# Local-attention weights and tables loaded once, inverse norms by log, exp and a Newton step, and a pipelined setup of the distance attention

## The chip, the core and the metric

The kernel runs on one core of one Trainium2 chip. The metric is the device time of one execution in microseconds (us). A core has a matrix engine (TensorE, PE in the rows; PEld are its weight loads), a vector engine (DVE), a scalar engine (ACT), GpSimd (POOL), and SyncE (SP), which here only issues DMA transfers. Each engine works its instructions off in order; between engines the order is kept by semaphores.

## What is computed

The reference applies seven stages to an activation x of 4 batches of 1024 rows of 128 numbers. In short:

```python
x = x + ffn(norm(x)) / 2        # gelu feed-forward, 512 hidden
x = x + distance_attention(norm(x))   # 16 heads of 8; scores = -|q_i - q_j|^2 / sqrt(8)
x = x + ffn(norm(x)) / 2
x = x + local(norm(x)) / 2      # two layers of windowed attention + gated feed-forward
x = x + causal_attention(norm(x))     # 16 heads of 64
x = x + local(norm(x)) / 2
# inside one local layer (8 heads of 64, windows of 64 rows):
q = l2norm(q) * qs; k = l2norm(k) * ks
q, k = rotary_xpos(q, k)
h = a * gelu(g); x = x + h @ w2 + b2
```

The l2norm needs 16 inverse square roots per row (8 heads of q, 8 of k). The rotation is linear, so the kernel multiplies by the inverse norm after it.

## The kernel before, in words

`macaron` runs the stages one after the other. x stays in SBUF as 32 tiles of 128 rows (`c.X`). Each stage consists of blocks; at the end of a block all engines meet in a barrier, and `clear` is a barrier too.

**Feed-forward** (`gelu_ffn`, L93, run twice). A first block issues four weight loads on SP (L131 to L134). `row_statistics` (L51) is a block of its own. The main block goes in 8 steps of 4 tiles. POOL adds half of the bias to x (L145), and its loop ends with the last step; DVE adds the product (L160) and takes the moments (L45, L48), which is the last work of the block.

**Distance attention** (`distance_attention`, L230). Its setup has these blocks: weight loads; row statistics; the normalised and transposed x (`normalised_columns`: DVE L90, PE L1343, ACT L1354); and a block that makes q in both orientations, split in a high and a low part, and the squared norms (PE L318 to L347, ACT L356 to L367, DVE L376 to L391), batch by batch. Only in the next block does SP stack the operands of a group of four heads: 40 DMAs (L435 to L439) copy 8-row strips of `q_hi`, `q_lo` and `n_hl` into `query` and `keys`. There are two such sets of buffers, for even and odd units, and 16 units (4 batches x 4 groups) in all. A unit has 32 jobs: two score matmuls each (L466), one Exp over 128x1024 on ACT (L530), and the products with v (L481).

**Local layers** (`local_layers`, L601, run twice). Each run has two layers and works 64 tiles in 16 groups of four. The order of work is written out by hand: `over_steps` goes through steps, a step has four ticks r = 0 to 3, and in each tick an engine works for tiles at several lags. `own` is the tile of this tick, `last` the one before, `scored` is two ticks back (TQ), `turned` three (PT), `out` four (OT); a group's feed-forward (`ffn`) comes two steps later, its last product (`ending`) three. In one tick and in this order

- PE: q/k products (L945), transposes of the rotated rows (L961), values (L954), projection (L1015), mask and scores (L971, L977), transposes of the probabilities (L989), weighted values (L1004). In r = 2 the feed-forward's transposes (L1026) and two thirds of its up-products (L1039), in r = 3 the last third and the transposes of the next group's rows (L934), in r = 0 the down-products (L1047).
- ACT: squares (L1128), attention out (L1155), qT and kT (L1137, L1138), values (L1132), the transposed probabilities (L1151), Exp (L1147). In r = 3 it begins with two Gelu gates (L1164), and after kT comes the third gate and the load of the Exp table (L1186); then values and hT (L1122), which PE needs for the next q/k products. The Gelu table is loaded at the end of r = 2 (L1201).
- DVE: sums of the probabilities and their inverse (L1244, L1246), rotation (L1226 to L1228), squared norms (L1231), residual (L1251), row maxima and subtraction (L1237, L1239). In r = 3 the gated products (L1264), in r = 0 the group's result (L1271) and its row moments (L1256, L1260).
- POOL: scaling of the probabilities (L857), scaling of the rotated rows of `last` (L850); in r = 1 the deviations (L863 to L877) and the bias b2 (L882); then cosine plus sine part (L889), the floor (L894) and the power -1/2 of the squared norms (L896) of `own`.

The power is one instruction:

```python
pool.tensor_tensor(inv_norm[:], floored[:], minus_half[:].broadcast_to([P, 2 * HEADS]), ALU.pow)
```

At the start of a run of the local layers, ACT issues the loads of angles, scales and mask (L1101 to L1104) and then writes the first eight normalised tiles (L1109). SP loads the shifted rows of the first group (L783, L784, L796) and behind them 14 weight arrays (L830 to L836). POOL and DVE multiply the two rotation tables (L921, L1300), DVE casts the mask (L1297). PE transposes the first group (L934), ACT copies it to hT (L1122), and PE, DVE, ACT and POOL wait for all weights before their first tick.

## Time and profile before

| | us |
|---|---|
| median of 3 runs | 3575.77 (3573.64 to 3576.94) |
| profiled execution | 3580.72 |
| its span, first to last instruction | 3578.6 |
| PE busy | 3183.2 (89%) |
| ACT busy | 2167.5 (61%) |
| DVE busy | 1976.4 (55%) |
| POOL busy | 1737.4 (49%) |
| mean granted TensorE clock | 0.959 |

The profile shows one execution. In its rows, times are us from the span's start unless they are marked ns. A row of the timeline gives start, duration, engine, line and operation, and in brackets the idle time before it and what ended that. The stages of that execution: first feed-forward to 87, distance attention to 677, second feed-forward to 752, local layers to about 1540, causal attention to 2768, local layers to the end. The reading is the same for both runs of the local layers.

### The profile page before, as it was taken

The page shows a single profiled execution, that of the slowest core. Times are in us where ns is not written, and L with a number is a line of the kernel's source. Part 1 is how long each engine was busy: PE and PEld are TensorE (multiplying, and loading weights), DVE is VectorE, ACT ScalarE, POOL GpSimd, SP SyncE. Part 2 cuts the span into 40 slices and gives each one's busy share as a digit, 9 for nine tenths or more (in the row PEclk, how much of TensorE's full clock was granted, in tenths as well). Part 3 has the DMA queues.
Part 4 walks back from the last instruction along what each step waited for, and adds up shares of the span by engine and source line. Part 5 has one row for each costly group of instructions (what it writes and reads, how often), then busy time and mean ns, then how long its engine had stood idle before and what let it go on. Part 6 is the DMA issues. An engine that isn't in the chain of part 4 may idle for free. (4 is left out here: it accounts for less than half of the span.)

```text
span 3578.6 us, 73165 instructions
## 1 busy us (share of the span) xinstructions
PE 3183.2 (89%) x26564; PEld 1951.8 (55%) x26564; DVE 1976.4 (55%) x4014; ACT 2167.5 (61%) x3580; POOL 1737.4 (49%) x1412
## 2 busy tenths in 40 slices
PE   6499999868999999749999999999998599999995
PEld 5222222435666666526666666666665366666663
DVE  4200000337777777545556555656565577777773
ACT  2399999526666666535555555555554366666663
POOL 1100000039889988523333333333332698998882
PEclk9699999979999999979999999999999799999998
DMA  1122222021111111100000000000000211111111
GB/s 33 20 36 39 36 38 38 7 74 34 35 36 38 37 36 34 25 10 9 7 6 9 6 9 6 9 6 9 6 6 4 86 37 35 37 37 37 35 33 36
DMA packets 124405, 95.70 MB, mean 27 GB/s; under 512 B 80448, under 2 KB 100544, under 8 KB 123968
## 3 DMA queue, kind: packets, MB, share of 16 engines
q1 hardware_dynamic: 122784, 89.41, 11.4%
q10 hardware_dynamic: 1440, 3.80, 0.3%
q8 instruction: 122, 2.00, 0.2%
q14 instruction: 59, 0.48, 0.0%
HBM read 22.90 MB, written 2.10 MB: 7 GB/s over the span
## 5 line engine op out<-in xcount | busy, mean ns | idle before, releaser
L1761 POOL TENSOR_SCALAR e<-e,inv 128x768 f32<-128x768 f32 (+7 forms) x512 | 375.3, 746 | 761.8 <-DVE inv L1653 761.8
L1724 ACT ACTIVATE e<-e,nmax 128x768 f32<-128x768 f32 (+7 forms) x512 | 395.4, 772 | 429.5 <-DVE e L1648 426.2
L1648 DVE TENSOR_SCALAR_CACHE_REDUCE e<-slot 128x768 f32<-128x768 f32 (+7 forms) x512 | 376.2, 754 | 243.8 <-PE slot L1537 243.8
L530 ACT ACTIVATE e<-slot 128x1024 f32<-128x1024 f32 x512 | 472.9, 1091 | 43.8 <-PE slot L466 43.8
L896 POOL TENSOR_TENSOR inv_norm<-floored,minus_half 128x16 f32<-128x16 f32 x128 | 374.1, 2922 | 10.7
L1641 DVE COPY eT<-slot 128x512 f32<-128x512 f32 (+3 forms) x384 | 238.7, 622 | 234.1 <-PE slot L1548 233.9
L1548 PE MATMUL slot<-ident,e 128*128 128x128 f32 x2304 | 332.7, 280 | 8.7 <-POOL e L1761 3.7
L1531 PE MATMUL slot<-key,q 64*128 64x512 f32 (+3 forms) x1536 | 318.1, 518 | 19.0 <-ACT v L1711 12.7
L889 POOL TENSOR_TENSOR rot<-cosine,sine 128x1024 f32<-128x1024 f32 x128 | 302.1, 2360 | 44.3 <-DVE sine L1228 44.3
L857 POOL TENSOR_TENSOR prob<-prob,inv_total 128x1024 f32<-128x1024 f32 x128 | 242.6, 1895 | 129.2 <-DVE inv_total L1246 129.2
L1548 PEld LDWEIGHTS slot<-ident,e 128*128 128x128 f32 x2304 | 252.5, 141 | 92.0 <-issue 68.9
L945 PE MATMUL slot<-w_qk,hT 128*128 128x512 f32 x512 | 254.5, 621 | 35.7 <-DMA b<-in_local_b_dram 17.8
L481 PE MATMUL slot<-e,v 128*32 128x512 f32 x2048 | 280.6, 621 | 0.4 <-ACT e L530 0.4
L1563 PE MATMUL slot<-eT,v 128*64 128x256 f32 x2048 | 254.6, 385 | 0.9 <-DVE X L1664 0.9
L1151 ACT ACTIVATE probT<-slot 128x1024 f32<-128x1024 f32 x128 | 131.0, 1023 | 200.8 <-PE slot L989 200.8
L466 PE MATMUL slot<-query,keys 36*128 36x512 f32 x1024 | 211.2, 478 | 45.6 <-DMA keys<-n_hl 31.8
L850 POOL TENSOR_TENSOR rot<-rot,inv_norm 128x1024 f32<-128x1024 f32 x128 | 243.4, 1901 | 0.3
L449 POOL COPY v<-q_all 128x256 f32<-128x256 f32 (+1 forms) x16 | 6.3, 401 | 479.6 <-PE slot L481 455.9
L466 PEld LDWEIGHTS slot<-query,keys 36*128 36x128 f32 x1024 | 88.8, 190 | 270.7 <-ACT e L530 219.7
L541 DVE COPY oT<-slot 128x512 f32<-128x512 f32 x32 | 22.1, 691 | 371.5 <-PE slot L481 371.5
L1226 DVE TENSOR_TENSOR cosine<-slot,tables 128x1024 f32<-128x1024 f32 x128 | 155.3, 1213 | 116.4 <-ACT sq L1128 83.6
L1128 ACT ACTIVATE sq<-slot 128x1024 f32<-128x1024 f32 x128 | 130.0, 1016 | 132.0 <-PE slot L945 132.0
(161 smaller groups left out, 6420.8 us busy)
## 6 DMA issues: line engine op xcount, KB each, us to landing
v_mix<-v SPq DMA_DIRECT2D x256, 128.0 KB, 2.3
w_qkv<-in_causal_w_dram SPq DMA_DIRECT2D x32, 192.0 KB
query<-q_hi SPq DMA_DIRECT2D x128, 32.0 KB
keys<-q_hi SPq DMA_DIRECT2D x128, 32.0 KB
query<-q_lo SPq DMA_DIRECT2D x128, 32.0 KB
keys<-q_lo SPq DMA_DIRECT2D x128, 32.0 KB
hs<-H SPq DMA_DIRECT2D x32, 128.0 KB
h1s<-H SPq DMA_DIRECT2D x32, 128.0 KB
```

The lines of the kernel that those rows point to most:

```text
L466: m = pe.matmul(out[:, h, :], keys[k][p][rows, t * P:(t + 1) * P], query[k][p][rows, half * 512:half * 512 + 512], start=True, stop=True)
L481: m = pe.matmul(c.slots[3][32 * j:32 * j + 32, half, :], v[k][:, t, j, :], e[(n - 1 + j // 2) % E_RING][:, j % 2 * 512:j % 2 * 512 + 512], ...
L530: act.activation(e[n % E_RING][:], c.slots[n % RING][:].rearrange(flat), ACT.Exp, scale=2 * SCALE).then_inc(e_ready, 1)
L889: pool.tensor_tensor(rot[:, a.j, :, :].rearrange(flat), cosine[:], sine[:], ALU.add).then_inc(rot_ready, 1)
L896: pool.tensor_tensor(inv_norm[:], floored[:], minus_half[:].broadcast_to([P, 2 * HEADS]), ALU.pow)\
L945: m = pe.matmul(bank_qk[:, half, :], hT[:, a.j * P:(a.j + 1) * P], w_qk[a.depth][:, half * 512:half * 512 + 512], start=True, stop=True)
L1531: pe.matmul(c.slots[h][:, bank, 0:hi - lo], q[k][rows, i * P:(i + 1) * P], key[k][rows, lo:hi], start=True, stop=True)
L1548: m = pe.transpose(turn[:, bank, t * P:(t + 1) * P], e[n % RING][h][:, (at + t) * P:(at + t + 1) * P], c.ident[:])
L1563: m = pe.matmul(o[64 * h:64 * h + 64, place(one) // 4, place(one) % 4 * P:(place(one) % 4 + 2) * P], v[k][:, t, 64 * h:64 * h + 64], eT[pa ...
L1648: dve.tensor_scalar(e[n % RING][h][:, 0:cols], c.slots[h][:].rearrange(flat)[:, 0:cols], -1.0, None, ALU.mult, ALU.min, accum_out=nmax[:, ...
L1724: act.activation(part, part, ACT.Exp, bias=nmax[:, n, h:h + 1], scale=-1.0, accum_out=total[:, n, h:h + 1]).then_inc(e_ready, 1)
L1761: pool.tensor_scalar(part, part, inv[:, n, h:h + 1], 1.0, ALU.mult, ALU.mult).then_inc(scaled, 1)
```

## The change

- The local weights, rotation tables and mask are allocated once (`local_weights`) and filled in the second call of `gelu_ffn`: four more DMAs on SP in its first block, twelve on SP in its main block, and on POOL, behind its loop, the two tables and the cast of the mask. Both runs of the local layers lose their loads, table products and waits for them.
- b2 is no longer added by POOL: an unused row of the hidden layer gets the constant 0.0625 * gelu(16) = 1, and the matching row of w2 holds b2.
- The inverse norms: POOL floors the squared norms of `own` as before. One tick later ACT takes Ln and then Exp(-x/2) of them, behind squares (and, for r < 3, behind attention out) and ahead of qT and kT; POOL makes one Newton step of four small instructions, each waiting for the one before, ahead of the scaling of the rotated rows. The table that is loaded behind the third gate and before the first tick is now the set named `natural_log_exp_and_others`. No load is written out ahead of Ln in r = 3.
- The setup of the distance attention normalises, transposes and multiplies in one block, batch by batch, and SP stacks the first unit's 40 strips in that block, as soon as the first batch's parts exist. The stacking of the second unit starts with the next block, without a wait, as before.

The diff, cut to its core:

```diff
+def load_local_weights(sp, w, d, loaded, count):
+
+    for l in range(len(w.w_qk)):
+        for dst, src in ((w.w_qk[l], "w_qk"), (w.w_v[l], "w_v"), (w.w_o[l], "w_o"), (w.w1[l], "w1"), (w.w2[l], "w2"),
+                         (w.small[l], "small")):
+            sp.dma_start(dst[:], d[src][l]).then_inc(loaded, 16)
+    sp.wait_ge(loaded, count)
...
+                if ahead:
+                    sp.dma_start(angles[:], c.const["angles"]).then_inc(tables_loaded, 16)
+                    for l in range(2):
+                        sp.dma_start(scales[l][:], ahead_d["scales"][l]).then_inc(tables_loaded, 16)
+                    sp.dma_start(band_f[:], c.const["band"]).then_inc(band_loaded, 16)
...
                 with pool.Fori(0, STEPS) as i:
                     pool.wait_ge(x_ready, i + 1)
                     pool.tensor_tensor(x_b2[:], c.X[:, bass.ds(i * G, G), :], bias, ALU.add).then_inc(x_b2_ready, 1)
+                if ahead:
+                    pool.wait_ge(tables_loaded, 48)
+                    wide = "p t x y d -> p t (x y d)"
+                    for l in range(2):
+                        pool.tensor_tensor(ahead.tables[l][:].rearrange(wide), angles[:].rearrange(wide),
+                                           scales[l][:].rearrange("p x y d -> p (x y d)").unsqueeze(1).broadcast_to([P, TPB, 256]),
+                                           ALU.mult).then_inc(ahead_ready, 1)
+                    pool.wait_ge(band_loaded, 16)
+                    pool.tensor_copy(ahead.band[:].rearrange("p a n -> p (a n)"), band_f[:].rearrange("p a n -> p (a n)"))\
+                        .then_inc(ahead_ready, 1)
+
+            if ahead:
+                @block.sync
+                def _(sp):
+                    load_local_weights(sp, ahead, ahead_d, ahead_loaded, 192)
...
+                @block.sync
+                def _(sp):
+                    heads = [stack_head(sp, stacked, 0, 0, j) for j in range(GROUP)]
+                    sp.wait_ge(cleared, 5)
+                    sp.wait_ge(hi_ready, 1)
+                    for high, _, _ in heads:
+                        high()
+                    sp.wait_ge(lo_ready, 1)
+                    for _, low, _ in heads:
+                        low()
+                    sp.wait_ge(norm_hi_ready, 1)
+                    sp.wait_ge(norm_lo_ready, 1)
+                    for _, _, norms in heads:
+                        norms()
...
+                    def turn_rows(i):
+                        pe.wait_ge(xn_ready, G * (i + 1))
...
+                        m.then_inc(turned, 1)
...
+                    pe.wait_ge(loaded, 80)
+                    pe.matmul(c.slots[2][:, 0, 0:P], wv[:], wk[:], start=True, stop=True).then_inc(cross_ready, 1)
+                    turn_rows(0)
+                    turn_rows(1)
+                    pe.wait_ge(merged_ready, 1)
+                    pe.matmul(c.slots[2][:, 1, 0:P], merged[:], wo[:], start=True, stop=True).then_inc(eff_ready, 1)
+                    for b in range(B):
+                        columns(b)
+                        if b < B - 1:
+                            turn_rows(2 * b + 2)
+                            turn_rows(2 * b + 3)
+                        rows(b)
+                        norms(b)
...
-                            norm_out(b - 1)
-                    norm_out(B - 1)
+                        if b < B - 1:
+                            columns(2 * b + 2)
+                            columns(2 * b + 3)
+                        act.wait_ge(norm_ready, b + 1)
+                        act.activation(n_hl[0:HEADS, b * S:(b + 1) * S], c.slots[2][0:HEADS].rearrange(flat),
+                                       ACT.Copy).then_inc(norm_hi_ready, 1)
+                        act.wait_ge(q_ready, b + 1)
+                        act.activation(q_all[:, b * TPB:(b + 1) * TPB, :, :].rearrange("p t h d -> p (t h d)"),
+                                       c.slots[0][:].rearrange(flat), ACT.Copy).then_inc(q_out, 1)
...
+                        dve.wait_ge(norm_hi_ready, b + 1)
...
-                def load_weights(l):
-                    sp.dma_start(w_qk[l][:], d["w_qk"][l]).then_inc(w_in_loaded[l], 16)
...
-                    sp.dma_start(small[l][:], d["small"][l]).then_inc(w_out_loaded[l], 16)
-                    sp.dma_start(b2[l][:], d["b2"][l]).then_inc(w_out_loaded[l], 16)
-
                 sp.wait_ge(cleared, 1)
                 load_hs(group(0, 0, None))
-                load_weights(0)
-                load_weights(1)
                 over_steps(sp, ticks)
...
+                def inverse_norms(a):
+
+                    first = first_inv[:, a.j % 2, :]
+                    pool.wait_ge(first_inv_ready, a.t + 1)
+                    if known(a.t, 1):
+                        pool.wait_ge(correction_ready, 2 * a.t)
+                    pool.tensor_tensor(inv_square[:], first, first, ALU.mult).then_inc(inv_square_ready, 1)
+                    pool.wait_ge(inv_square_ready, a.t + 1)
+                    if known(a.t, 1):
+                        pool.wait_ge(inv_norm_ready, a.t)
+                    pool.tensor_tensor(product[:], inv_square[:], floored[:, a.j % 2, :], ALU.mult).then_inc(correction_ready, 1)
+                    pool.wait_ge(correction_ready, 2 * a.t + 1)
+                    pool.sem_inc(correction_seen, 1)
+                    pool.tensor_scalar(correction[:], product[:], -0.5, 1.5, ALU.mult, ALU.add).then_inc(correction_ready, 1)
+                    pool.wait_ge(correction_ready, 2 * a.t + 2)
+                    if known(a.t, 2):
+                        pool.wait_ge(unit_ready, a.t - 1)
+                    pool.tensor_tensor(inv_norm[:, a.j % 2, :], correction[:], first, ALU.mult).then_inc(inv_norm_ready, 1)
+
                 def unit_rows(a):
                     pool.wait_ge(inv_norm_ready, a.t + 1)
                     pool.wait_ge(rot_ready, a.t + 1)
                     rows = rot[:, a.j, :, :]
-                    pool.tensor_tensor(rows, rows, inv_norm[:].unsqueeze(2).broadcast_to([P, 2 * HEADS, D]), ALU.mult)\
+                    pool.tensor_tensor(rows, rows, inv_norm[:, a.j % 2, :].unsqueeze(2).broadcast_to([P, 2 * HEADS, D]), ALU.mult)\
                         .then_inc(unit_ready, 1)
...
-                def inverse_norms(a):
+                def floor_norms(a):
                     pool.wait_ge(norm2_ready, a.t + 1)
                     pool.sem_inc(floor_ready, 1)
-                    pool.tensor_scalar(floored[:], norm2[:, a.j % 2, :], 1e-24, None, ALU.max).then_inc(floor_ready, 1)
-                    pool.wait_ge(floor_ready, 2 * a.t + 2)
-                    pool.tensor_tensor(inv_norm[:], floored[:], minus_half[:].broadcast_to([P, 2 * HEADS]), ALU.pow)\
-                        .then_inc(inv_norm_ready, 1)
+                    if known(a.t, 2):
+                        pool.wait_ge(correction_ready, 2 * a.t - 2)
+                        pool.sem_inc(floor_ready, 1)
+                    else:
+                        pool.sem_inc(floor_ready, 1)
+                    pool.tensor_scalar(floored[:, a.j % 2, :], norm2[:, a.j % 2, :], 1e-24, None, ALU.max).then_inc(floor_ready, 1)
 
                 def ticks(step, depth):
                     for r in range(G):
                         if turned := tile(step, r, PT, depth):
                             scale(turned)
                         if last := tile(step, r, 1, depth):
+                            inverse_norms(last)
                             unit_rows(last)
                         if r == 1 and (ffn := group(step, FFN, depth)):
                             deviations(ffn)
-                            add_b2(ffn)
                         if own := tile(step, r, 0, depth):
                             rotated(own)
-                            inverse_norms(own)
+                            floor_norms(own)
...
-                pool.wait_ge(tables_loaded, 48)
...
                 pool.wait_ge(cleared, 4)
-                pool.wait_ge(w_out_loaded[0], 80)
-                pool.wait_ge(w_out_loaded[1], 80)
                 over_steps(pool, ticks)
...
                 t1(group(0, 0, None))
-                pe.wait_ge(band_ready, 1)
-                for l in range(DEPTH):
-                    pe.wait_ge(w_in_loaded[l], 32)
-                    pe.wait_ge(w_out_loaded[l], 80)
                 over_steps(pe, ticks)
...
-                act.dma_start(angles[:], c.const["angles"]).then_inc(tables_loaded, 16)
-                for l in range(DEPTH):
-                    act.dma_start(scales[l][:], d["scales"][l]).then_inc(tables_loaded, 16)
-                act.dma_start(band_f[:], c.const["band"]).then_inc(band_loaded, 16)
...
+                def inverse_norms(a):
+                    act.wait_ge(floor_ready, 3 * a.t + 3)
+                    act.activation(log_norm2[:], floored[:, a.j % 2, :], ACT.Ln).then_inc(log_norm2_ready, 1)
+                    act.wait_ge(log_norm2_ready, a.t + 1)
+                    if known(a.t, 2):
+                        act.wait_ge(inv_norm_ready, a.t - 1)
+                    act.activation(first_inv[:, a.j % 2, :], log_norm2[:], ACT.Exp, scale=-0.5).then_inc(first_inv_ready, 1)
...
                             squares(own)
                         if r < 3 and out:
                             attention_out(out)
+                        if last := tile(step, r, 1, depth):
+                            inverse_norms(last)
                         if scored:
                             heads(scored)
                         if r == 3 and ffn:
                             gates(ffn, 2)
-                            act.preload_act_table(ACT.Exp)
+                            act.preload_act_table_set("natural_log_exp_and_others")
                         if own:
...
-                act.preload_act_table(ACT.Exp)
-                for l in range(DEPTH):
-                    act.wait_ge(w_out_loaded[l], 80)
+                act.preload_act_table_set("natural_log_exp_and_others")
                 over_steps(act, ticks)
...
                     if known(a.t, 2):
-                        dve.wait_ge(inv_norm_ready, a.t - 1)
+                        dve.wait_ge(floor_ready, 3 * a.t - 3)
                     dve.tensor_reduce(norm2[:, a.j % 2, :], sq[:].rearrange("p (h d) -> p h d", d=D), AX.X, ALU.add)\
...
-                dve.wait_ge(band_loaded, 16)
-                dve.tensor_copy(band[:].rearrange(flat), band_f[:].rearrange(flat)).then_inc(band_ready, 1)
-                dve.wait_ge(tables_loaded, 48)
...
-                for l in range(DEPTH):
-                    dve.wait_ge(tables_ready[l], 1)
-                    dve.wait_ge(w_out_loaded[l], 80)
                 over_steps(dve, ticks)
...
+    bias[:, 0, hid], bias[:, 1, hid] = 0.0625, 16.0
     down = np.zeros((n, chunks * P, P), w2.dtype)
-    down[:, :hid] = w2
+    down[:, :hid], down[:, hid] = w2, b2
...
-        gelu_ffn(nc, c, d["ffn_w1"], d["ffn_b1"], d["ffn_w2"], d["ffn_b2"])
-        local_layers(nc, c, local, moments=False)
+        weights = local_weights(nc, st, c)
+        gelu_ffn(nc, c, d["ffn_w1"], d["ffn_b1"], d["ffn_w2"], d["ffn_b2"], weights, local)
+        local_layers(nc, c, weights, moments=False)
         causal_attention(nc, c, d["causal_gain"], d["causal_shift"], d["causal_w"], d["causal_wo"], d["causal_bias"])
-        local_layers(nc, c, local)
+        local_layers(nc, c, weights)
```

## Rows read from the trace of the kernel before

**Rows 1.** Windows: busy time of each engine; one steady step, two ramp stretches of two ticks.
```profile
core 0: us, PE busy (x) PEld busy (x) DVE busy (x) ACT busy (x) POOL busy (x), PEclk, DMA share, GB/s
3166.10:3210.30 44.20, 41.76 (x430) 28.64 (x429) 33.73 (x48) 28.44 (x41) 39.78 (x26) 1.00 0.16 38
...
2845.30:2863.90 18.60, 15.56 (x191) 10.88 (x189) 14.97 (x18) 11.17 (x18) 18.43 (x12) 1.00 0.15 33
2863.90:2882.40 18.50, 17.33 (x198) 12.38 (x199) 13.99 (x18) 11.12 (x18) 18.33 (x11) 1.00 0.13 30
```

**Rows 2.** Timeline of PE in the steady step from 3166.1.
```profile
3170.03 0.66 PE L1026 MATMUL slot<-ident,z 128*128 128x128 f32 x4 [1.07 <-DVE H L1251]
3171.39 1.09 PE L989 MATMUL slot<-ident,prob 128*128 128x128 f32 x8 [0.71 <-POOL prob L857]
...
3177.43 1.95 PE L945 MATMUL slot<-w_qk,hT 128*128 128x512 f32 x4 [0.42 <-DVE hid L1264]
...
3186.49 1.96 PE L945 MATMUL slot<-w_qk,hT 128*128 128x512 f32 x4
```

**Rows 3.** Timeline of ACT in r = 3 of that step.
```profile
3182.01 0.69 ACT L1164 ACTIVATE gate<-slot,small 128x512 f32<-128x512 f32 x1 [0.59 <-PE slot L1039]
3182.72 1.28 ACT L1186 ACT_TABLE_LOAD   x1
3184.01 0.60 ACT L1132 ACTIVATE v<-slot 128x512 f32<-128x512 f32 x1
3185.81 0.60 ACT L1122 ACTIVATE hT<-slot 128x512 f32<-128x512 f32 x1 [1.20 <-PE slot L934]
```

**Rows 4.** Groups of POOL's instructions in the steady step 3122.0 to 3166.1.
```profile
L896 POOL TENSOR_TENSOR inv_norm<-floored,minus_half 128x16 f32<-128x16 f32 x4 | 11.7, 2924 | 0.3
L889 POOL TENSOR_TENSOR rot<-cosine,sine 128x1024 f32<-128x1024 f32 x4 | 9.4, 2359 | 0.0
...
L882 POOL TENSOR_TENSOR H<-H,b 128x512 f32<-128x512 f32 x1 | 1.3, 1277 | 0.0
...
L894 POOL TENSOR_SCALAR floored<-norm 128x16 f32<-128x16 f32 x4 | 1.0, 255 | 0.1
```

**Rows 5.** Timeline of ACT before the first local run: its nearest small instruction.
```profile
753.71 0.32 ACT L81 ACTIVATE deviation<-moments,eps 128x32 f32<-128x32 f32 x1
```

**Rows 6.** Timeline of the start of the first local run.
```profile
757.45 3.19 ACT L1109 ACTIVATE H<-X,x_shift,rstd 128x128 f32<-128x128 f32 x8 [3.41 <-issue]
...
771.11 0.60 ACT L1122 ACTIVATE hT<-slot 128x512 f32<-128x512 f32 x1 [10.48 <-PE slot L934]
...
780.06 3.75 PE L945 MATMUL slot<-w_qk,hT 128*128 128x512 f32 x4 [8.99 <-DMA b<-in_local_b_dram]
```

**Rows 7.** Timeline of the setup of the distance attention.
```profile
95.69 2.14 PE L1343 MATMUL slot<-ident,xn 128*128 128x128 f32 x8 [10.80 <-DVE xn L90]
...
105.68 0.77 PE L318 MATMUL slot<-wk,wv 128*128 128x128 f32 x2 [1.35 <-PEq L38]
...
136.55 1.21 DVE L384 TENSOR_TENSOR n_hl<-slot,n_hl 16x1024 fp32r<-16x1024 f32 x1 [4.35 <-ACT n_hl L356]
138.52 0.89 SPq L435 DMA_DIRECT2D query<-q_hi  x1
...
165.44 0.51 SPq L439 DMA_DIRECT2D keys<-n_hl  x1
...
167.26 1.65 PE L466 MATMUL slot<-query,keys 36*128 36x512 f32 x6 [31.79 <-DMA keys<-n_hl]
```

**Rows 8.** Windows of the distance attention, shortly after its start and later.
```profile
180.00:187.00 7.00, 7.00 (x32) 1.71 (x34) 0.00 (x0) 4.40 (x5) 0.00 (x0) 0.50 0.26 40
...
250.00:300.00 50.00, 48.49 (x340) 14.85 (x332) 4.78 (x12) 49.63 (x54) 0.80 (x2) 1.00 0.24 37
```

**Rows 9.** Timeline of the second feed-forward's end and the table product.
```profile
743.30 1.29 POOL L145 TENSOR_TENSOR x_b<-X,half_b 128x512 f32<-128x512 f32 x1 [6.16 <-DVE X L160]
...
752.41 1.28 ACT L78 ACT_TABLE_LOAD   x1 [5.88 <-PEq L38]
...
761.45 4.49 POOL L921 TENSOR_TENSOR tables<-angles,scales 128x2048 f32<-128x2048 f32 x1 [4.76 <-DMA scales<-in_local_scales_dram]
```

More of the change, by code:

```diff
@@ L90, in normalise, with local_weights, sb, gelu_ffn @@
     return dve.tensor_scalar(dst, c.X[:, t, :], c.moments[:, t, 0:1], c.rstd[:, bass.ds(t, 1)], ALU.subtract, ALU.mult)
-def gelu_ffn(nc, c, w1_d, b1_d, w2_d, b2_d):
+def local_weights(nc, st, c, depth=2):
+    HEADS, D, CH = 8, 64, 3
+    w = Ctx()
+    def sb(name, shape, dt=F32):
+        return st.enter_context(nc.sbuf_tensor(c.fresh(name), shape, dt))
+    w.w_qk = [sb(f"w_qk{l}", [P, 2 * HEADS * D]) for l in range(depth)]
+    w.w_v = [sb(f"w_v{l}", [P, HEADS * D]) for l in range(depth)]
+    w.w_o = [sb(f"w_o{l}", [P, HEADS // 2, P]) for l in range(depth)]
+    w.w1 = [sb(f"w1{l}", [P, 2, CH, P]) for l in range(depth)]
+    w.w2 = [sb(f"w2{l}", [P, CH, P]) for l in range(depth)]
+    w.small = [sb(f"small{l}", [P, 8]) for l in range(depth)]
+    w.tables = [sb(f"tables{l}", [P, TPB, 2, 2, D]) for l in range(depth)]
+    w.band = sb("band", [P, 2, 512], BF16)
+    return w
+def load_local_weights(sp, w, d, loaded, count):
[4 more added lines that the diff above has]
+    sp.wait_ge(loaded, count)
+def gelu_ffn(nc, c, w1_d, b1_d, w2_d, b2_d, ahead=None, ahead_d=None):
     HID = 512
@@ L125, in gelu_ffn @@
         moments_ready = sem("ffn_moments_ready")
+        if ahead:
+            angles = sb("angles", [P, TPB, 2, 2, 64])
+            scales = [sb(f"scales{l}", [P, 2, 2, 64]) for l in range(2)]
+            band_f = sb("band_f", [P, 2, 512])
+            tables_loaded = sem("tables_loaded")
+            band_loaded = sem("band_loaded")
+            ahead_loaded = sem("ahead_loaded")
+            ahead_ready = sem("ahead_ready")
         with nc.Block() as block:
@@ new lines, in norms @@
+                    def norms(b):
+                        pe.wait_ge(sq_ready, b + 1)
+                        if b:
+                            pe.wait_ge(norm_hi_ready, b)
+                            pe.wait_ge(norm_lo_ready, b)
+                        else:
+                            pe.wait_ge(merged_ready, 1)
+                            pe.wait_ge(eff_out, 1)
+                        for half in range(2):
+                            m = pe.matmul(c.slots[2][0:HEADS, half, :], sel[:], sq[b % 2][:, half * 512:half * 512 + 512],
+                                          start=True, stop=True)
+                        m.then_inc(norm_ready, 1)
@@ L359, in _ @@
+                    columns(0)
+                    columns(1)
                     for b in range(B):
[L360 to L362 removed]
                         act.wait_ge(qT_ready, b + 1)
```

172 lines of the change are left out of this document (77 added, 95 removed).

## The prediction

> **What bounds the kernel now.** The windows come first. In a steady step of the local layers PE is busy 41.76 of 44.20 us, POOL 39.78, ACT 28.44 [rows 1]. So PE leads, POOL follows closely, and at most 2.4 us a step can be won without taking work off PE. PE's timeline says what ends its idle times: 1.07 us by DVE's residual, 0.71 by POOL's scaling of the probabilities, 0.42 by the gated product [rows 2]; the rest, 0.24, by ACT. In the ramp (ticks 2 to 8, no feed-forward yet) two ticks take 18.5 to 18.6 us and POOL fills 18.4 of them, PE 15.6 and 17.3 [rows 1]: there POOL is the bound. The groups of POOL show why: the power costs 2.92 us a tile, 11.7 a step, for 16 numbers a row [rows 4]. Last come ACT's rows of r = 3, because the change puts work there: from the third gate to hT it has 0.59 and 1.20 us of idle time, and hT is done at 3186.41, right before PE's next q/k products at 3186.49 [rows 2, 3]. That copy is on the path, and has no slack beyond those 1.79 us.
>
> **Steady step, what goes.** POOL loses the power (11.7) and b2 (1.28) and gets 16 small instructions. The nearest row is the floor, 0.255 us on the same 128x16, and the next starts 0.08 after it: 0.335 each, 1.34 a tile, 5.4 a step. POOL falls to about 32 of 44 us. Of PE's waits only the 0.71 goes. The 1.07 stays: the residual of r = 2 sits behind the rotation, which waits for POOL's sum of r = 1, and there POOL begins when DVE hands it the inverse totals, with no power in between; b2's 1.28 leaves that stretch and 1.34 of Newton enters it. The 0.42 follows PE's own products through Exp, table load and gate, and stays. Gain 0.71.
>
> **Steady step, what comes.** In r = 3 ACT has the Gelu table when it meets Ln, and no load is written out for it; one has to be placed. Then Exp, then the third gate with Gelu again, then the named set. The edit names the set that holds both functions twice, which suggests that a function asked for by itself brings another: a load ahead of Ln, one ahead of Exp, one ahead of the gate. Three more loads of 1.28 [rows 3] and two small ACTIVATEs; these the trace does not show. Their bounds are nothing and the 0.42 or so of a wide one; the nearest row is 0.32 for 128x32 [rows 5]; I take 0.22 each. Together 3.84 + 0.44 = 4.3 us between squares and hT. The idle 1.79 absorbs its part, so hT is 2.5 us late; the transposes of the next rows are no way around it, since on DVE the residual waits behind the third gated product, which is late with the gate. PE waits for hT, and everything behind it in the step follows from PE. Minus the 0.71: +1.8 us a step. There are 14 steps a run with a feed-forward and own tiles, the last without a successor: 27 in all, +49 us. For r < 3 the two small instructions lie ahead of qT and kT, where ACT has idle time of their size (no price); if it had none, 3 x 0.44 would go on each step, which the range holds.
>
> A load is followed at once by the next ACTIVATE: 3182.72 + 1.28 = 3184.00, values at 3184.01 [rows 3]. The Trainium skill (ScalarE: Activation LUTs, What ACT_TABLE_LOAD costs) adds to the 1283 ns a drain of about 1380 ns for each switch of sets. By that rule the three loads would cost 8.0 us instead of 3.8; the row shows no such gap.
>
> **Ramp.** POOL per tick without the power and with Newton: 9.2 - 2.9 + 1.3 = 7.6 us. PE needs (15.56 + 17.33) / 4 = 8.2 [rows 1]; with the hops that remain, 8.5. Against 9.28 that is 0.8 a tick; 7 to 8 ticks a run, two runs: -12 us (0 if a chain between engines binds at once, -20 if PE's 8.2 falls too).
>
> **Start of a run of the local layers.** hT is complete at 771.71, the first q/k product runs at 780.06, held by the last weight array [rows 6]: 8.3 us go. ACT's first normalised tile stands behind the issue of four DMAs (3.41 us idle by issue, of which x_shift would hold it for half): 1.7 earlier. 10 us a run, the second alike: -20 (-16 to -24). PE is cold there before and after.
>
> **Second feed-forward, where the work goes.** SP issues four more loads in the first block, and a barrier waits for SP. The 40 stacking issues take 27.4 us, 0.69 each [rows 7]; plain ones are shorter, I take 2 us in all (0 to 2.8). The twelve weight loads lie beside 60 us of steps: nothing; should they be uncovered, a 10 us queue is what the old start showed. POOL's loop ends at 744.6; two tables at 4.49 and a cast (between 0.3 and the 2.36 of a two-operand instruction of its size [rows 4]; 1.4) end at 755.0. The block now ends near 751.7, 0.7 before the table load at 752.41 [rows 9]: +3.3 (+2 to +5). Sum +5.
>
> **Distance setup.** Now: transposes from 95.69, the next block from 105.68 to 137.76, 40 issues from 138.52 to 165.95, scores at 167.26 [rows 7]. Afterwards SP issues beside the products: q_hi of batch 0 exists about 8 to 9 us after 95.7, plus 27.4 gives 132. The engines need 32.1 us (the old block) plus between nothing and 32 x 0.27 = 8.6 for the transposes inside: 128 to 136. I take 133, barrier 0.8, scores at 134: -33 (-27 to -39). The second unit's stacking starts at 134 as well and needs 27.4 + 1.3; the first unit lasts 32 x 0.93 = 29.8 [rows 8]: just covered, so no further gain or loss. The long idle of PE (31.8) left it at the lower of its two levels, 1.2 GHz, until 187: five Exps in 7 us against 0.93 each later [rows 8], some 6 us lost. With a pause of 3 us left this may or may not go: half, -3. Sum -36. Moving b2 into w2 uses a padded row: nothing.
>
> **Sum.** -36 + 5 - 20 - 12 + 49 = -14. The profiled execution took 3580.7 (span 3578.6 and 2.1 around it), so 3567; it lies 5 above the median shown, and against 3575.8 that gives 3562.
>
> **Rivals.**
> 1. *Fewer loads.* If one load serves Ln and Exp, a step grows by 0.5: -14 - 27 x 1.28 = -49, 3527. If none is needed (a set that holds all, or ordering I misread), each step gains 0.71: -14 - 49 - 19 = -82, 3494. For: nothing in the trace of before shows which set Exp alone gets. Against: Gelu and Exp already cost two loads a step.
> 2. *Slower: the added chain is dearer than its instructions.* Each of the four Newton instructions waits for the one before. At 0.5 instead of 0.335 Newton takes 2.0, 0.7 more than b2 gave back on the path of r = 1; with Ln and Exp at 0.42, hT is later by another 0.4. Then a step grows by 2.9, 27 x 1.1 = 30 more: 3592. From a growth of 14 / 27 = 0.5 above my 1.8, at 2.3 a step, the change loses. For: nothing in the trace has four dependent small instructions. Against: the hop of 0.08.
> 3. *The drain of the skill's rule.* 3 x 1.38 x 27 = +112: 3674. The rows at two places a step show none.
> 4. *The setup's gain does not come*, because SP's strips or the second unit's stacking hold PE: -14 + 36 = +22, 3598.
>
> **How the numbers follow.** Forecast with three loads 0.54, its own range 3545 to 3582; one load for both 0.14; none 0.05; dear chain 0.18; setup held 0.07; drain 0.02. About 0.2% (7 us) can be told from no change. Of the forecast's 0.54, 0.37 lie below -7, 0.12 within it, 0.05 above. Faster: 0.37 + 0.14 + 0.05 = 0.56. Same: 0.12 and 0.06 of the dear chain, 0.18. Slower: 0.26. The range leaves out the case without loads, the drain and the tails: 3520 to 3600.
>
> **What would show it.** Right: three more table loads of 1.28 in each steady step, ahead of Ln, Exp and the third gate; hT right before the q/k products and PE's longest wait of the step there; steps of 46 us instead of 44.2; POOL near 32 a step; ticks of the ramp near 8.5; scores of the distance attention at 134; the first local q/k product 10 us after its block's start earlier than now, and the second feed-forward 5 us longer. Wrong: steps below 44 (fewer loads, or r = 3 has slack that I do not see), steps above 46.7, or Newton's four instructions taking over 1.8 us.

## The result and the profile after

| | before | after |
|---|---|---|
| median | 3574.65 (3573.64 to 3576.94, 6 runs) | 3559.87 (3558.11 to 3567.53, 6 runs) |
| ratio | | 0.9957 [0.9947, 0.9967] |
| span of the profiled execution | 3578.6 | 3556.3 |
| PE, DVE busy | 3183.2, 1976.4 | 3178.3, 1968.0 |
| ACT, POOL busy | 2167.5, 1737.4 | 2314.3, 1442.1 |

The change saves 14.8 us by the medians. The two profiled executions differ by more (spans 3578.6 and 3556.3), because the one of before took some 6 us more than its median and the one of after some 2 less. POOL loses 295 us of work, ACT gains 147. The sum is small because three gains (setup, b2, weights) and one large loss (the new norms) nearly cancel. All line numbers from here on are of the kernel after, unless a row is said to be of another.

The loads come first. ACT's groups after, over the whole span (group | busy us, mean ns | idle before):

```profile
L1310 ACT ACT_TABLE_LOAD x32 | 41.1, 1283 | 0.6
L1295 ACT ACT_TABLE_LOAD x32 | 41.1, 1283 | 0.6
L1250 ACT ACT_TABLE_LOAD x28 | 35.9, 1283 | 0.5
L1254 ACT ACT_TABLE_LOAD x28 | 35.9, 1283 | 0.5
L1271 ACT ACT_TABLE_LOAD x28 | 35.9, 1283 | 0.5
```

L1310 and L1295 are the two loads that the kernel before had too. Three more stand in each of 28 steps: at Ln, at Exp and at the third gate. ACT's timeline of r = 3 after, which answers to [rows 3]:

```profile
3143.79 1.03 ACT L1227 ACTIVATE sq<-slot 128x1024 f32<-128x1024 f32 x1 [1.51 <-PE slot L1053]
3144.84 1.28 ACT L1250 ACT_TABLE_LOAD   x1
3146.13 0.22 ACT L1250 ACTIVATE log_norm<-floored 128x16 f32<-128x16 f32 x1
3146.36 1.28 ACT L1254 ACT_TABLE_LOAD   x1
3147.66 0.21 ACT L1254 ACTIVATE first_inv<-log_norm 128x16 f32<-128x16 f32 x1
...
3148.86 1.28 ACT L1271 ACT_TABLE_LOAD   x1
3150.16 0.69 ACT L1271 ACTIVATE gate<-slot,small 128x512 f32<-128x512 f32 x1
3150.86 1.28 ACT L1295 ACT_TABLE_LOAD   x1
3152.16 0.60 ACT L1231 ACTIVATE v<-slot 128x512 f32<-128x512 f32 x1
3152.65 0.59 ACT L1221 ACTIVATE hT<-slot 128x512 f32<-128x512 f32 x1
```

ACT has no idle time from the load ahead of Ln to hT; the gaps of 0.59 and 1.20 us of before are used up. What PE waits for in the same step, from its timeline, which answers to [rows 2] (rows with a wait; one of 0.24 for ACT's attnT is left out, before and after alike):

```profile
3133.26 0.60 PE L1079 MATMUL slot<-band,ident_bf 128*128 128x512 bf16 x2 [0.66 <-ACT kT L1237]
3135.36 0.63 PE L1134 MATMUL slot<-ident,z 128*128 128x128 f32 x4 [0.46 <-DVE H L1358]
3141.80 1.96 PE L1053 MATMUL slot<-w_qk,hT 128*128 128x512 f32 x4 [0.16 <-DVE hid L1371]
3148.90 0.60 PE L1079 MATMUL slot<-band,ident_bf 128*128 128x512 bf16 x2 [0.81 <-ACT kT L1237]
3151.88 0.66 PE L1042 MATMUL slot<-ident,hs 128*128 128x128 f32 x4 [1.34 <-DVE H L1358]
```

The largest are in r = 3 and stand where the loads are: kT behind two of them (0.81), and the transposes for hT behind VectorE's residual (1.34), which stands behind the late third gate. The 0.71 for the probabilities is gone and the 1.07 has shrunk to 0.46. The wait of 0.66 in r = 2 is new, and comes up again below. POOL's busy time in a step fell from 39.78 [rows 1] to 30.37, as the windows show (columns as in [rows 1]):

```profile
3118.50:3164.30 45.80, 42.13 (x429) 28.57 (x428) 33.81 (x48) 33.52 (x51) 30.37 (x37) 1.00 0.15 35
```

The period of a step, from one result of a group on DVE (`H<-slot,H 128x512`) to the next, is the measure for everything below. It is the mean of the 26 full steps of an execution: 44.59 us before, 46.12 after.

The distance setup after, which answers to [rows 7], from the timeline (SPq rows are DMA issues):

```profile
104.72 0.91 SPq L329 DMA_DIRECT2D query<-q_hi  x1
...
130.98 0.50 SPq L339 DMA_DIRECT2D keys<-n_hl  x1
...
135.18 1.65 PE L584 MATMUL slot<-query,keys 36*128 36x512 f32 x6 [3.46 <-PEq L38]
```

And PE's clock around it, in the windows that answer to [rows 8]:

```profile
135.00:140.00 5.00, 3.89 (x12) 1.75 (x12) 0.00 (x0) 4.84 (x5) 0.74 (x2) 0.50 0.25 37
140.00:150.00 10.00, 10.00 (x60) 2.40 (x58) 0.00 (x0) 8.51 (x10) 0.00 (x0) 0.76 0.27 40
150.00:160.00 10.00, 10.00 (x68) 3.25 (x68) 0.99 (x3) 10.00 (x12) 0.00 (x0) 1.00 0.28 44
```

The granted clock was 1.00 from 125 to 131 us, where PE was busy 5.91 of 6 us, and 0.95 on the mean from 131 to 135. So even in a pause of 3.46 us PE came down to the lower level (0.50, 1.2 GHz), but the higher one was back some 10 us after the first score and not 20 as before.

The second feed-forward's end and the first start, which answer to [rows 6, 9], from the timelines of POOL, ACT and PE:

```profile
708.13 1.27 POOL L185 TENSOR_TENSOR x_b<-X,half_b 128x512 f32<-128x512 f32 x1 [6.18 <-DVE X L215]
709.36 8.98 POOL L190 TENSOR_TENSOR tables<-angles,scales 128x2048 f32<-128x2048 f32 x2
718.29 1.03 POOL L194 CAST band<-band_f 128x1024 bf16<-128x1024 f32 x1
```
```profile
720.11 1.28 ACT L78 ACT_TABLE_LOAD   x1 [8.73 <-PEq L38]
```
```profile
736.98 3.78 PE L1053 MATMUL slot<-w_qk,hT 128*128 128x512 f32 x4 [0.69 <-ACT hT L1221]
```

Put together, the profiled executions give this account. The marks are the last score, DVE's last product in the second feed-forward (749.80 before, 714.63 after), ACT's table load behind it, the first q/k product of each run (the second at 2803.96 and 2763.04), and the first and last group result of each run.

| stretch | measured, us | predicted, us |
|---|---|---|
| start to the last score of the distance attention | -35.8 | -36 |
| to the table load behind the second feed-forward | +3.5 | +5 |
| to the first q/k product of local run 1 | -10.8 | -10 |
| filling, to the first group result, run 1 | -4.2 | -6 |
| its steps | +21.1 | +24.5 |
| causal attention and the start of run 2 | -14.7 | -10 |
| filling, run 2 | -1.7 | -6 |
| its steps to the end | +20.3 | +24.5 |
| sum | -22.3 | -14 |

Of the 14.7, 11.0 lie between run 2's `deviation` on ACT and its first q/k product; the rest is spread over unchanged code. One execution is a draw for such stretches: the first score with the old setup came at 163.7 to 167.3 us in four profiles, with the new one at 134.8 to 140.1 in nine.

### The profile page after: what moved, and what is told of

The parts are those of the page before. It is cut to its first block and busy times, and to the rows that moved or that the text cites. A ratio compares the mean times of both kernels' runs of the same rounds, so it can differ in the third digit from the quotient of the medians.

```text
span 3556.3 us, 74663 instructions
## 1 busy us (share of the span) xinstructions
PE 3178.3 (89%) x26564; PEld 1944.6 (55%) x26564; DVE 1968.0 (55%) x4010; ACT 2314.3 (65%) x3920; POOL 1442.1 (41%) x1765
## 5 line engine op out<-in xcount | busy, mean ns | idle before, releaser
L648 ACT ACTIVATE e<-slot 128x1024 f32<-128x1024 f32 x512 | 472.5, 1087 | 11.8 <-PE slot L584 11.7
L1814 ACT ACTIVATE eT<-slot 128x512 f32<-128x512 f32 (+3 forms) x384 | 163.6, 426 | 74.2 <-PE slot L1644 72.6
L1351 DVE TENSOR_REDUCE total<-prob 128x8 f32<-128x1024 f32 x128 | 154.9, 1210 | 83.0 <-ACT prob L1246 83.0
```

Source lines behind the costliest of these rows:

```text
L648: act.activation(e[n % E_RING][:], c.slots[n % RING][:].rearrange(flat), ACT.Exp, scale=2 * SCALE).then_inc(e_ready, 1)
```

## The experiments

Each kernel is the one named with one edit, timed in rounds beside the kernel before. Theory at the start: the loss is the three table loads in r = 3, through hT; Newton's work takes b2's place on POOL. All periods are means of 26 steps. The step's differences are read within profiles and carry no interval of their own; the ratios do.

| kernel | median, us | ratio to before | step, us |
|---|---|---|---|
| before, four sets of runs | 3574.7 to 3576.1 | | 44.59 |
| after | 3559.87 | 0.9957 [0.9947, 0.9967] | 46.12 |
| e1 Ln and Exp behind the third gate | 3496.05 | 0.9773 [0.9757, 0.979] | 43.70 |
| e2 named set loaded ahead of Ln | 3527.92 | 0.9871 [0.9855, 0.9888] | 44.77 |
| e3 power on GpSimd again | 3483.92 | 0.975 [0.9734, 0.9767] | 43.06 |
| e4 old setup | 3589.78 | 1.0046 [1.0029, 1.0063] | 46.07 |
| e5 = e1, rotation first on POOL | 3477.71 | 0.9724 [0.9708, 0.9741] | 42.87 |
| e6 = e3, rotation first on POOL | 3499.31 | 0.9787 [0.977, 0.9805] | 43.58 |
| e7 before, b2 in w2 only | 3530.51 | 0.9873 [0.9856, 0.9889] | 43.02 |
| e8 before, weights ahead only | 3555.89 | 0.994 [0.9923, 0.9956] | 44.61 |
| e9 = e5, unit rows before the floor | 3474.42 | 0.9717 [0.9701, 0.9733] | 42.70 |
| e10 after, b2 on POOL again | 3605.78 | 1.0082 [1.0066, 1.0099] | 47.63 |
| e11 after, memsets later | 3560.71 | 0.9955 [0.9938, 0.9972] | 46.09 |

### The table loads: e1 and e2

```diff
@@ e1: ACT's ticks
-                        if last := tile(step, r, 1, depth):
+                        last = tile(step, r, 1, depth)
+                        if r < 3 and last:
                             inverse_norms(last)
...
                             act.preload_act_table_set("natural_log_exp_and_others")
+                        if r == 3 and last:
+                            inverse_norms(last)
@@ e2: ACT's ticks, ahead of inverse_norms(last)
+                            if r == 3 and ffn:
+                                act.preload_act_table_set("natural_log_exp_and_others")
```

> In r = 3, Ln and Exp of the inverse norms move on ACT behind the third gate and its table load, so no load has to be placed for them or ahead of the gate. Theory (three loads on the way to hT set the step): the three loads vanish from every steady step (28 each at three places, 84 in all), the step falls from 45.8 us to 43.5 to 43.9, and 27 steps give -50 to -60 against the changed kernel: 3500 to 3510 us. Rival (the Newton chain on POOL is what makes the step long): the loads vanish, but the step stays above 45 and the time within 15 of 3560, since POOL now gets the norms of r = 3 no earlier than before.

> The set with both functions is loaded by name ahead of Ln in r = 3: two added loads a step instead of three. Theory (the slack of 1.79 us on ACT is used up, each further load is paid in full): 1.28 x 27 = 35 less than the changed kernel, 3525 us, step 44.5. Rival (the step is limited by something beside ACT, the third load is partly hidden): less than 15 us gained.

e2 leaves two added loads of three and gains 32 us, 1.35 a step for a load of 1.28. e1 leaves none and gains 64, 2.42 a step. e2 held; in e1 the step held and the total came out 4 us below its range. In e1 the two small functions find their set loaded; ACT's timeline of its r = 3:

```profile
3148.01 0.69 ACT L1271 ACTIVATE gate<-slot,small 128x512 f32<-128x512 f32 x1 [0.59 <-PE slot L1147]
3148.71 1.28 ACT L1296 ACT_TABLE_LOAD   x1
3150.01 0.21 ACT L1250 ACTIVATE log_norm<-floored 128x16 f32<-128x16 f32 x1
3150.25 0.21 ACT L1254 ACTIVATE first_inv<-log_norm 128x16 f32<-128x16 f32 x1
3150.37 0.58 ACT L1231 ACTIVATE v<-slot 128x512 f32<-128x512 f32 x1
3151.81 0.60 ACT L1221 ACTIVATE hT<-slot 128x512 f32<-128x512 f32 x1 [0.86 <-PE slot L1042]
```

Three loads of 1.28 (3.85) cost 2.42: the difference is the idle time in r = 3 that they filled, which shows again as 0.59 and 0.86. The Trainium skill (ScalarE: Activation LUTs, Table sets: the hidden batching unit) counts one load for Ln followed by Exp. With the set named, e2 agrees: the load at L1291 (28 times) serves both. With the functions asked for alone, the kernel after shows two.

### The norms as a whole: e3

```diff
@@ POOL, floor_norms (not shown: ACT's inverse_norms and Newton's four instructions go, and the Exp table is loaded in place of the named set)
+                    pool.wait_ge(floor_ready, 2 * a.t + 2)
+                    pool.tensor_tensor(inv_norm[:, 0, :], floored[:, 0, :], minus_half[:].broadcast_to([P, 2 * HEADS]), ALU.pow)\
+                        .then_inc(inv_norm_ready, 1)
```

> The changed kernel with the inverse norms by the power on POOL again; the new setup, the weights ahead and b2 in w2 stay. Theory (the new norms cost 49 in the steps and give 12 in the ramp): 37 less than the changed kernel, 3523 us, steady step 44.1 or a little below since b2's 1.28 us on POOL are gone, ramp ticks 9.3. Rival (Ln, Exp and Newton are worth their place, the gain of the change comes from them): above 3560.

It missed by 39 us: 3483.92. The step is 43.06, 1.53 under the kernel before, though POOL still computes its powers. So something else that stayed in e3 was worth 1.5 us a step, and the new norms cost 76 us in all, 12 of them even without a load (e1 against e3). Only b2 was left as a cause in the steps.

### What b2 was worth: e7 and e10

```diff
@@ e7: POOL's ticks of the kernel before; e10 puts the same lines back into the kernel after
-                            add_b2(ffn)
@@ DVE, out
-                    dve.wait_ge(b2_ready, a.g + 1)
@@ local_layout
-    down[:, :hid] = w2
+    down[:, :hid], down[:, hid] = w2, b2
```

> The kernel before with one edit: the bias b2 comes into the second weight product as a row, and GpSimd's addition of b2 to the slot and its wait are gone. Theory (the addition of 1.28 us stood in GpSimd's chain of r = 1 that TensorE waits for, so it was worth its whole time in each of the 27 steps of a steady stretch, 35 us): 3540 us. The account behind the prediction, in which GpSimd had room for it once its place was free: within 10 us of the time before, 3565 to 3575 us.

> The kernel after with one part undone: b2 is added to the slot by GpSimd in r = 1 again, behind the deviations and ahead of the rotation. Chain account (whatever stands there delays the rotation, VectorE's residual and TensorE by its whole length, with Newton's four instructions ahead of it as without them): 1.3 to 1.6 us a step, 3595 to 3602 us. Rival (the three table loads set the step now, and the chain on GpSimd has room behind them): within 10 us of the kernel after, 3560 to 3570 us.

e7 gains 45.6 us, 1.57 a step on the mean, 10 us more than the chain account said and far from the other one. In most of the steps the gain is close to the 1.28 of the addition: 1.2 to 1.3 us in seven of the 13 of run 1, 1.4 to 1.5 in four. In the first and the twelfth it is 2.8, and the traces were not followed there. In e7's r = 1 POOL's rotation stands directly behind the deviations. Of the kernel before, DVE's rotation in r = 2 shows the link, a wait of its own of 0.71 for POOL's sum of r = 1; in e7 DVE's same instruction has no such wait:

```profile
3166.23 1.22 DVE L1226 TENSOR_TENSOR cosine<-slot,tables 128x1024 f32<-128x1024 f32 x1 [0.71 <-POOL rot L889]
```

PE's rows with a wait in e7's step (its own line numbers): of [rows 2], the 1.07 is now 0.23 and the 0.71 is 0.31, together 1.24 less. The 0.42 is as before.

```profile
3126.90 0.66 PE L1018 MATMUL slot<-ident,z 128*128 128x128 f32 x4 [0.23 <-DVE H L1243]
3127.86 1.09 PE L981 MATMUL slot<-ident,prob 128*128 128x128 f32 x8 [0.31 <-POOL prob L856]
3133.89 1.95 PE L937 MATMUL slot<-w_qk,hT 128*128 128x512 f32 x4 [0.42 <-DVE hid L1256]
```

The way back is as dear: e10 costs 45.9 us over the kernel after, 4 more than the upper end expected, in spite of the three loads (it also loads the two arrays of b2 again, beside the second feed-forward). The wait it lengthens is the new one of r = 2, from 0.66 to 1.77:

```profile
3124.42 0.60 PE L1088 MATMUL slot<-band,ident_bf 128*128 128x512 bf16 x2 [1.77 <-ACT kT L1246]
```

The chain is the same with a new end. POOL's floor stands behind the rotation, ACT's Ln waits for the floor (1.24 in the kernel after, 2.36 in e10), and qT and kT stand behind Ln on ACT. ACT's and POOL's rows of the kernel after:

```profile
3131.77 0.22 ACT L1250 ACTIVATE log_norm<-floored 128x16 f32<-128x16 f32 x1 [1.24 <-POOL floored L1012]
```
```profile
3123.87 0.22 POOL L952 TENSOR_TENSOR inv_square<-first_inv 128x16 f32<-128x16 f32 x1
3124.17 0.22 POOL L956 TENSOR_TENSOR product<-inv_square,floored 128x16 f32<-128x16 f32 x1
3124.58 0.20 POOL L959 TENSOR_SCALAR correction<-product 128x16 f32<-128x16 f32 x1 [0.20 <-POOL product L956]
3124.97 0.22 POOL L963 TENSOR_TENSOR inv_norm<-correction,first_inv 128x16 f32<-128x16 f32 x1 [0.18 <-POOL correction L959]
3125.28 1.90 POOL L969 TENSOR_TENSOR rot<-rot,inv_norm 128x1024 f32<-128x1024 f32 x1
...
3129.03 2.36 POOL L1002 TENSOR_TENSOR rot<-cosine,sine 128x1024 f32<-128x1024 f32 x1
3131.48 0.26 POOL L1012 TENSOR_SCALAR floored<-norm 128x16 f32<-128x16 f32 x1
```

### POOL's order: e5, e6 and e9

```diff
@@ e5: POOL's ticks, on top of e1 (e9 also puts unit_rows(last) ahead of floor_norms(own))
+                        if own := tile(step, r, 0, depth):
+                            rotated(own)
                         if last := tile(step, r, 1, depth):
                             inverse_norms(last)
+                        if own:
+                            floor_norms(own)
+                        if last:
                             unit_rows(last)
                         if r == 1 and (ffn := group(step, FFN, depth)):
                             deviations(ffn)
-                        if own := tile(step, r, 0, depth):
-                            rotated(own)
-                            floor_norms(own)
```

> The late-logarithm kernel (3496 us) with GpSimd's work of a later step in another order: the sum of the rotation comes before the four Newton instructions of the last repeat, and the floor of the own norms before the unit rows. Nothing else differs. Theory (what is left of the price of the new norms is GpSimd's chain in r = 1: four Newton instructions of about 0.33 us each stand ahead of the rotation, which VectorE's residual waits for, and the floor that the logarithm waits for, the waits of 0.66 and 0.46 us in r = 2): both waits go, a steady step falls from 43.8 to about 43.0 us, and the whole is 3475 to 3485 us. Rival (the unit rows, which now come 1.3 us later, are what the transposes wait for, or GpSimd was not the bound): 3496 us or more.

> The kernel with the power on GpSimd (3484 us) with its rotation's sum ahead of the unit rows and the floor ahead of the power. Theory (GpSimd's order in r = 1 still delays VectorE's residual a little, the wait of 0.23 us for the third residual): 3470 to 3480 us. Rival (nothing on TensorE's path waits for GpSimd's order any more): 3484 us, no change; if the power's later place delays the attention's scores that wait for it, above 3490 us.

> The kernel with the late logarithm and the rotation first (3478 us), with one more exchange on GpSimd: the unit rows come before the floor of the own norms (0.25 us). Theory (in r = 2 of a steady step TensorE waits 0.67 us for the unit rows, and they follow the floor directly): 0.25 us of it goes in each step, 3470 to 3475 us. Rival (the floor, 1.9 us later, makes the logarithm late, and ScalarE holds the copies of q and k behind it): 3485 us or more.

e5 held, 3477.71, 0.83 us a step under e1: both waits of r = 2 that it named are gone, and one of 0.67 for the unit rows has come. With the power on POOL the same order loses (e6, 3499.31): the rival's second branch has the number right, but not the reason. PE's wait for the scaled probabilities is 0.65 where e3 has 0.32. The power's later place is not what makes it: in both orders the same POOL instructions, the power among them, stand between one scaling of the probabilities and the next. In e6 the rotation comes first and POOL idles 0.30 ahead of it for DVE's sine part, so that from scaling to scaling it takes 11.65 us instead of 11.31. POOL's and PE's rows of e6, then PE's of e5:

```profile
3082.74 2.36 POOL L1002 TENSOR_TENSOR rot<-cosine,sine 128x1024 f32<-128x1024 f32 x1 [0.30 <-DVE sine L1331]
```
```profile
3094.14 1.09 PE L1095 MATMUL slot<-ident,prob 128*128 128x128 f32 x8 [0.65 <-POOL prob L976]
```
```profile
3116.93 1.09 PE L1071 MATMUL slot<-ident,rot 128*128 128x128 f32 x8 [0.67 <-POOL rot L969]
```

e9 exchanges 0.25 us and comes out at 3474.42, 3.3 us lower and inside what was expected. The intervals of the two ratios overlap, so the gain rests on the traces: the wait for the unit rows is 0.46 instead of 0.67, and the step 0.17 shorter. It is the fastest kernel of the study: 2.8% under before, 2.4% under after. So the change's way to make the norms beats the power where both were tried, by 9.5 us (e9 against e3), once its loads and its place in POOL's order are mended. Its steady step (windows) has less than 1 us left beside PE's own work:

```profile
3116.92:3159.28 42.36, 41.54 (x428) 28.59 (x428) 33.61 (x49) 29.64 (x49) 30.46 (x36) 1.00 0.17 39
```

### Setup and weights: e4 and e8

e4 takes the new setup out of the kernel after; e8 puts only the block ahead (four more loads on SP, fourteen weight loads with b2's two, POOL's two tables and the cast) into the kernel before.

> The changed kernel with the setup of the distance attention of before. Theory (the setup gives 33 by its start and some 3 by the clock): 36 more than the changed kernel, 3596 us, first scores near 168. Rival (the stacking only moves and binds later): less than 20 more.

> The kernel before with one edit: the local runs' weights, tables and mask are loaded and made once, beside the second feed-forward; the distance setup, the power and the addition of b2 stay. By the prediction's terms: 20 us off the two starts and 5 us on the second feed-forward, so about 3560 us. Rival (the starts are covered by TensorE's own clock rising and by other setup): no change, 3575 us.

The setup is worth 29.9 us, 6 less than expected. The score marks of all profiles agree with it. The first score comes at 165.9 (mean of four) against 137.1 (nine), 28.8 earlier, and the last one 31.2 earlier. The 35.8 of the pair before and after was a good draw for the new one. The weights are worth 20.3, 5 more than expected. Setup 29.9, b2 45.6 to 45.9 and weights 20.3 add up to about 96, against 91.5 measured for e3, which has all three. With the new norms' 76 taken off those 91.5, the 15 us of the result remain.

### A side observation: e11

```diff
@@ POOL, first block of the distance setup
                 def _(pool):
+                    pool.wait_ge(xn_ready, 4 * G)
                     for k in range(2):
```

> The kernel after with one wait added on GpSimd in the distance setup: its ten memsets (about 1 us each) start when VectorE has normalised the first 16 tiles, and not beside them. Theory (the memsets beside it made VectorE's normalising of eight tiles take 4.16 and 4.08 us where it took 2.14 us in the kernel before): both groups take 2.1 to 2.3 us again; the memsets and the first copies come later by 1 to 3 us, so the whole stays within 4 us of the kernel after, 3557 to 3565 us. Rival (the slow groups have another cause, such as the two halves of the buffer): they stay at 4.1 us.

DVE's rows of the kernel after, then of e11:

```profile
93.77 4.16 DVE L90 TENSOR_SCALAR xn<-X,moments,rstd 128x128 f32<-128x128 f32 x8 [0.73 <-PEq L38]
...
99.77 4.08 DVE L90 TENSOR_SCALAR xn<-X,moments,rstd 128x128 f32<-128x128 f32 x8
```
```profile
94.01 2.14 DVE L90 TENSOR_SCALAR xn<-X,moments,rstd 128x128 f32<-128x128 f32 x8 [1.01 <-PEq L38]
...
97.99 2.13 DVE L90 TENSOR_SCALAR xn<-X,moments,rstd 128x128 f32<-128x128 f32 x8
```

The theory held: beside the memsets the same eight instructions took twice as long. The total stayed where it was (3560.71). The first copy is issued at 104.72 in both profiles; in e11 it stands behind the fifth memset, which ends at 104.70, so what DVE wins is not passed on.

## Why the prediction was right

The mechanism of the loss, three table loads on the way to hT, was right and is shown by e1 and e2. That the total came within 2 us is partly luck: the steps cost less than taken, the filling and the setup gave less, the weights gave more, and these errors of 5 to 8 us partly cancel. The forecast gave b2 no worth of its own, and that was its largest mistake.

**Steady steps, what comes: right.** Three loads at the three named places, small functions at 0.21 to 0.22 as taken, 1.79 us of idle time used up. Taken: 2.5 us a step for all of it. Measured: 2.42 (after against e1) for the loads, with the small functions in both kernels. PE's longest waits were in r = 3, as forecast, but one stage ahead of hT's consumer: at the transposes (1.34) and the scores (0.81), not at the q/k products.

**What goes: the sum right, the terms not.** Predicted was a loss of the 0.71 only, with b2's 1.28 and Newton's 1.34 changing places in the chain of r = 1 at no gain. Measured: b2 gives 1.57 a step, Ln, Exp and Newton in place of the power take back 0.64 (e1 against e3), so 0.93 stays instead of 0.71. Newton is as long as thought (1.32 for the four, 1.41 to the next instruction), but only 0.86 of it is busy time, and so POOL is busy for 30.4 us a step and not 32. Why it costs less than b2 there was not tested by itself; that POOL reaches the probabilities earlier without the power would account for it (PE's wait for them is gone). Added up, -0.93 + 2.42 = +1.49, which is what the step shows (+1.53); taken was +1.8. The step missing from the prediction is the wait of r = 2: Ln waiting for POOL's floor with kT behind it. The prediction priced Ln and Exp for r < 3 at nothing because ACT has idle time there, and did not ask what they wait for; that wait is 0.66, and taking it away with its neighbour gave 0.83 a step (e5 against e1). The same oversight in another form spoiled the expectation of e3: b2 was held to be worth nothing by itself, though the prediction's own chain said that whatever leaves that stretch counts in full.

**Drain: refuted.** The prediction gave it 2 in 100. By the Trainium skill (ScalarE: Activation LUTs, What ACT_TABLE_LOAD costs) each switch has 1380 ns behind the 1283. The trace shows 1283 ns and the next instruction within 0.02 us (3146.36 + 1.28, then 3147.66), and a load taken away gave back 1.35, not 2.66.

**Filling: too large.** -6 instead of -12 in the profiles. No run was made for this stretch. Seven ticks, from the fourth q/k product to the eleventh, took 65.3 and 65.6 us before and 62.4 in both runs after: 8.9 a tick where 8.5 was taken, a gain of 0.4 instead of 0.8. The three ticks ahead of them ran partly at the lower clock and moved by -1.2 in run 1 and +1.1 in run 2. After the change POOL idles 5.5 us in 37 us of filling of run 2 (2815 to 2852), all of it waiting for DVE's inverse totals; so POOL is no longer the bound there, and a chain through DVE is the likely one.

**Starts and feed-forward: right.** Starts -10.8 and -11.0 (taken -10 each), feed-forward +3.5 (taken +5): +2.9 at POOL's tail and +0.6 in all that lies ahead of it, the issues among it.

**Setup: right in size, 6 us on the high side.** In the profiled pair the scores come 32 earlier, close to the 33 worked out; on the mean of all profiles it is 28.8, 4 less. From the first score to the last the new setup takes 481.3 us on the mean and the old one 483.7, 2.4 less against the 3 taken for the clock, but single profiles scatter by 8, so this term stays open. The high level did come back earlier after the short pause, but the lower one was still granted.

**Rivals.** Fewer loads: not in the kernel after, and e2 and e1 show the two cases at -32 and -64 us (from the prediction's 3562: 35 and 68). Dear chain: Newton's instructions cost 0.35 each with their hops (1.41 for the four), and the step stayed under the deciding 2.3. Setup held: no.

## What to carry to other kernels

Where an engine switches between table sets, count the loads in the trace and name the set where two functions share one; then put small functions behind a switch that exists already (here 64 us). Before pricing work moved off a busy engine, find the stretch of its order that another engine waits for: 1.28 us of an addition inside it were worth 45 us, and 11.7 us of powers a step, which at their best place were only 0.36 us a step dearer than the new norms (e3 against e9), little. When a small instruction is put on an engine with idle time, ask what it waits for and what is queued behind it.

## What was not expected of the hardware

DVE's normalising instructions (128x128, f32, SBUF to SBUF) came at one in 0.52 us beside POOL's memsets and at one in 0.27 without them, and seven of the ten memsets took 1.09 to 1.10 instead of 0.95: two DVE instructions passed in the time of one memset. e11 shows that the memsets are the cause. The Trainium skill (SBUF — State Buffer, Who interferes with whom) says that VectorE, in a mode with two ports that `tensor_scalar` can enter, and GpSimd contend for a shared pair of ports, which the first to issue holds for its whole instruction. That both engines slow down agrees with it; no run here shows the mode or the ports. PE fell to its lower level within a pause of 3.46 us, which the prediction left open, and had the higher level back some 10 us after the first score.
